# Layer 0 of a four-layer graph transformer: weight staging spread further, offset rows one product earlier, the experts' norm by chunks, and the experts' offsets in one fp16 product

## The chip, the cores and the metric

One core of one Trainium2 chip runs the whole program as one launch. The metric is the device time of that core in microseconds; lower is better. Times of the kernel are given as a median of runs, and one further execution was profiled.

## What is computed

Four layers run over x, 1250 rows (graph nodes) of 512 values, with 20000 edges. Each layer adds a graph part and an attention part to x, and then a mixture of experts. Only layer 0 is touched here:

```
xn = _layernorm(x, axis=-1)
x = x + _L0_gnn_ref(xn, edge_index, W, b) + _L0_mix_ref(xn[None], ...)[0]
x = x + _L0_ffn_ref(_layernorm(x, axis=-1)[None], ...)[0]

# _L0_mix_ref, for i in range(2):
    y = layernorm(x, ln1_g[i], ln1_b[i])
    ...                                   # attention with exponential features
    x = x + o @ Wo[i] + bo[i]
    y = layernorm(x, ln2_g[i], ln2_b[i])
    h = gelu(y @ W1[i] + b1[i])           # 512 -> 2048
    x = x + h @ W2[i] + b2[i]             # 2048 -> 512

# _L0_ffn_ref, 8 experts of 512 -> 128 -> 512, top 2, and one shared expert 512 -> 512 -> 512
scores = softmax(xf @ gate_w.T)
combine = top 2 of scores, normalised     # (tokens, 8)
eo = relu(xf @ w1 + b1) @ w2 + b2
y = einsum('te,teh->th', combine, eo)     # holds combine @ b2, the experts' offsets
shared = relu(xf @ sw1 + sb1) @ sw2 + sb2
```

## The kernel before

The 1250 rows lie as T = 10 tiles of 125 rows, and the tiles form three chunks, of 4, 4 and 2 tiles (CH). Each engine has its own program, written out by hand in the order in which it runs; semaphores connect them. A product in fp32 precision is made of three fp16 products, high x high, high x low and low x high (PARTS), so each operand is split into a high and a low fp16 half. `gemm_N` gives rows (12 matmuls of 512 columns for each tile, 120 in all, line L498), `gemm_T` gives columns (144 matmuls of 500 or 250 columns, line L480). TensorE (PE) writes into rings of three PSUM banks: the ring "act" is emptied by ScalarE (ACT), the ring "dve" by VectorE (DVE).

**Weights.** A weight matrix of 512x512 is a unit. SyncE (SP) loads it in four quarters into one of two `raw` slots, and GpSimd (POOL) splits each quarter (scale L2655, cast L2657, subtract L2659) into one of two unit slots. Unit u may be split when unit u-2 has been used. In layer 0: unit 4 is Wo of the first depth, 5 to 12 are its W1 and W2 in four pairs (b = 0 to 3), 16 is Wo of the second depth, 17 to 24 its W1 and W2; 25 to 28 are the experts' first and second matrices, four experts in a unit, 29 and 30 the shared expert's; 31 and on belong to layer 1.

**Staging.** The 50 expert units of layers 1 to 3 are split in the same way, ahead of time, and written back to memory: after unit u POOL splits SPLIT_AFTER[u] such units into four staging buffers in AT, and SP stores them. Since POOL works in program order, whatever is staged after unit u comes before the split of unit u+1. When the last is stored, SP brings the graph's adjacency back into AT (`adj_back`, 3.1 MB), which the gather of layer 1 reads; its loads stand in SP's queue ahead of the next unit's loads.

```
SPLIT_AFTER = {4: 9, 5: 9, 16: 9, 17: 9}
SPLIT_AFTER.update({u: 1 for u in [6, 7, 8, 9, 10, 11] + [18, 19, 20, 21, 22, 23, 24, 25]})
```

**End of each depth.** `add_to(M, "m_ffn", ...)` on DVE adds each bank of a gemm_N to the running stream M (L1850). In the last of the four (b = 3) it also adds the offset row b2 (L1853), in the second depth it adds M to X (L2140), and it takes the statistics of the row norm (L1793); after the last tile of a chunk DVE aggregates, ACT takes the root (L1395), DVE gives the scales. In the first depth (`beside_tiles`) PE transposes the first chunk ahead of tile 8 of the last product. Ahead of the experts it does not: `transposes_T` (L430) stands after the whole product, and on ACT `ln_root(Y)` norms all three chunks (L1426) before `evac_direct` empties the first bank (L1351). ACT copies the high halves (`hi_D`), DVE makes the low halves (`lo_D`, L1837).

**Experts.** PE multiplies three banks of unit 25, then the gate logits, then the rest. DVE turns the logits into `comb` in some 25 small steps (`gates`). PE transposes `comb` (10 transposes), and ten fp32 matmuls, combT (8 rows) times the offset rows E0, give the experts' offsets (L885), each emptied by DVE (`add_to(X, "read_dve")`, L1850). Then follows gemm_N with unit 26, whose banks come from the same ring of three.

Of the kernel before, what the change touches and what calls it, by code (L numbers as in the profile page):

```python
# [13 lines left out]
N = 1250  # L14
# [66 lines left out]
SEL = 9  # L81
MAX16 = 2048
# [5 lines left out]
def build(nc, x_in, src_in, dst_in, units_in, moe_in, be1_in, cols_in, rows_in, eb_in, gb2_in, proj_in, out):  # L88
    ctx = ExitStack()
    with ctx:  # L90
# [119 lines left out]
        combT = K[0:NE, N:2 * N]  # L210
# [173 lines left out]
        def _(pe):  # L384
# [49 lines left out]
            def normed_columns(c):  # L434
# [3 lines left out]
                for k in range(KC):  # L438
# [4 lines left out]
                    ins.then_inc(sem("filled_act"), 1)  # L443

# [248 lines left out]
            for dep in range(2):  # L693
# [107 lines left out]
                for b in range(4):  # L801
# [11 lines left out]
                    if b == 3:  # L813
                        uses_row()
# [3 lines left out]
                    else:  # L818
                        gemm_N("Q", lambda k, g: w[:, g, k, :], "m_ffn", by_chunk=True, between=beside_tiles if b == 3 and dep == 0 else None)
# [50 lines left out]
            def expert_biases(row):  # L870
# [3 lines left out]
                for t0, nt in CH:  # L874
                    pe.wait_ge(*left("act"))
                    o = bank("act", "combT")
                    for j in range(nt):
                        ins = pe.transpose(o[0:8, j * R:(j + 1) * R], comb3[:, t0 + j, :], ident[0:R, 0:R])
# [197 lines left out]
            transposes_T(lambda t, a, b: nat(Y, t, a, b), "normed", "lo_D")  # L1076
# [239 lines left out]
        def _(act):  # L1316
# [315 lines left out]
            def combT_evac():  # L1632
                for t0, nt in CH:
                    evac("act", "combT", combT[:, t0 * R:(t0 + nt) * R], nt * R, p=8)


            ln_root(Y)
            evac_direct("YT")
# [116 lines left out]
        def _(dve):  # L1755
# [268 lines left out]
            for dep in range(2):  # L2024
# [103 lines left out]
                for b in range(4):  # L2128
# [6 lines left out]
                    def stream_done(t):  # L2135

                        if dep == 0:
                            stream_rows(t)
                        else:
                            tt(nat(X, t), nat(X, t), nat(M, t), ALU.add).then_inc(sem("dve_step"), s.one("dve_step"))  # L2140
                            dve.wait_ge(*s.latest())
                            ln_scales(X, t)
                    add_to(M, "m_ffn", f"b2{dep}" if b == 3 else None, after=stream_done if b == 3 else None)
# [171 lines left out]
            def gates(probs, pair_softmax, gbias=False):  # L2315
# [45 lines left out]
                else:  # L2361
# [5 lines left out]
                    step(tt(comb3, w1, bc(mr), ALU.mult), "comb")  # L2367
                    step(ts(combs[0:R, :], comb[0:R, :], WS, None, ALU.mult))

# [8 lines left out]
            low_direct("YT")  # L2378
# [3 lines left out]
            row_free("E0")  # L2382
# [589 lines left out]
```

## Time and profile before

| | us |
|---|---|
| median of 3 runs | 3175.11 (3169.66 to 3175.34) |
| the profiled execution, its own time | 3171.26 |
| its span, first to last instruction | 3169.5 |
| TensorE busy | 2704.7 (85%) |
| VectorE busy | 1708.1 (54%) |
| GpSimd busy | 1193.4 (38%) |
| ScalarE busy | 1125.9 (36%) |
| mean granted TensorE clock | 0.921 of full speed |

The span is what the trace covers; 1.8 us of the execution's time lie around it. Busy shares are means over the whole span: an engine with 38% can still be the one that is waited for in one stage.

### The profile page before, as it was taken

The numbers are of one execution on the slowest core, as the hardware profiler recorded it, in microseconds if no ns is written. First come the engines' busy times: TensorE is split into PE (matmuls) and PEld (weight loads), VectorE is DVE, ScalarE is ACT, GpSimd is POOL, SyncE is SP. The second block draws the span as 40 slices with busy tenths as digits, with TensorE's granted clock in tenths as the row PEclk, the third lists the DMA queues.
The fourth block names the chain that finished last, engine by engine and source line by source line (L and its number), as shares of the span: only waits on it lengthen the run. The fifth ranks groups of instructions, "written<-read, shape, count | busy, mean of one in ns | idle before, by whom it ended". The sixth has DMA issues, their size and how long they took to land. (4 is left out here: it accounts for less than half of the span.)

```text
span 3169.5 us, 46348 instructions
## 1 busy us (share of the span) xinstructions
PE 2704.7 (85%) x17011; PEld 1760.6 (56%) x17011; DVE 1708.1 (54%) x3454; ACT 1125.9 (36%) x2510; POOL 1193.4 (38%) x1445
## 2 busy tenths in 40 slices
PE   8999899799889889899986956999599958589784
PEld 4655668456558646455544635777355645355453
DVE  8875878434678833655527253222435466541543
ACT  3254466233447522313214323444332235320132
POOL 2031677885377788623212212111003226300042
PEclk9999899999999999989997977999799979798887
DMA  2011445442154444411100007999601059600198
GB/s 63 1 51 37 126 144 160 139 130 80 47 153 147 153 134 131 136 33 34 37 11 27 31 15 286 416 417 414 200 4 38 21 210 322 211 14 0 33 365 271
DMA packets 163941, 415.35 MB, mean 131 GB/s; under 512 B 23931, under 2 KB 75675, under 8 KB 140236
## 3 DMA queue, kind: packets, MB, share of 16 engines
q1 hardware_dynamic: 149213, 362.10, 33.6%
q0 software_dynamic: 12960, 42.48, 3.5%
q10 hardware_dynamic: 1555, 7.95, 1.0%
q8 instruction: 132, 2.16, 0.3%
q14 instruction: 81, 0.66, 0.1%
HBM read 325.37 MB, written 87.09 MB: 130 GB/s over the span
## 5 line engine op out<-in xcount | busy, mean ns | idle before, releaser
L2655 POOL TENSOR_SCALAR raw<-raw 128x512 f32<-128x512 f32 x380 | 271.6, 715 | 1085.8 <-PE ps L480 434.7
L498 PE MATMUL ps<-units,ARENA 128*125 128x512 f16 x2880 | 643.9, 385 | 35.0 <-POOL units L2659 25.6
L480 PE MATMUL ps<-ARENA,units 128*128 128x500 f16 (+1 forms) x2952 | 537.5, 344 | 19.6 <-ACT tmp L1415 9.4
L498 PEld LDWEIGHTS ps<-units,ARENA 128*125 128x125 f16 x2880 | 391.1, 138 | 274.6 <-POOL units L2659 26.1
L480 PEld LDWEIGHTS ps<-ARENA,units 128*128 128x128 f16 x2952 | 289.2, 98 | 265.6 <-issue 19.0
L1813 DVE TENSOR_TENSOR ARENA<-tmp,ARENA 128x500 f16<-128x500 f32 (+3 forms) x241 | 173.1, 723 | 360.8 <-ACT ARENA L1341 187.6
L2659 POOL TENSOR_TENSOR AT<-raw,AT 128x512 f16<-128x512 f32 x200 | 243.9, 1220 | 17.0
L1340 ACT ACTIVATE tmp<-ps,cols 128x500 f32<-128x500 f32 (+1 forms) x156 | 95.7, 613 | 395.1 <-PE ps L480 385.3
L2703 POOL DMA_INDIRECT ARENA<-rows_d,proj x81 | 80.0, 987 | 389.0 <-DVE ARENA L2200 363.0
L2659 POOL TENSOR_TENSOR units<-raw,units 128x512 f16<-128x512 f32 x180 | 217.6, 1209 | 15.3
L2708 POOL DMA_INDIRECT picks_d<-ARENA,proj x81 | 82.1, 1014 | 345.1 <-DVE ARENA L2240 344.5
L973 PE MATMUL ps<-ARENA 128*128 128x128 f16 x3240 | 191.7, 220 | 0.1
L973 PEld LDWEIGHTS ps<-ARENA 128*128 128x128 f16 x3240 | 187.4, 98 | 1.5 <-DVE ARENA L2231 0.6
L988 PE MATMUL ps<-ARENA 128*128 128x512 f16 x810 | 184.2, 380 | 0.0
L1850 DVE SCALAR_TENSOR_TENSOR ARENA<-ps,ARENA 125x512 f32<-125x512 f32 x100 | 68.7, 687 | 153.6 <-PE ps L498 153.4
L430 PE MATMUL ps<-ident,ARENA 125*128 125x125 f32 x280 | 53.1, 352 | 111.8 <-DVE ARENA L1837 33.5
L1594 ACT ACTIVATE tmp<-ps,proj 128x128 f32<-128x128 f32 x270 | 102.6, 380 | 102.8 <-PE ps L973 72.7
L2657 POOL CAST AT<-raw 128x512 f16<-128x512 f32 x200 | 132.9, 664 | 12.8
L613 PE MATMUL ps<-ARENA 125*125 125x500 f16 (+1 forms) x588 | 118.6, 353 | 10.9 <-DVE ARENA L1915 9.9
L988 PEld LDWEIGHTS ps<-ARENA 128*128 128x128 f16 x810 | 74.8, 98 | 95.1 <-issue 12.2
L2240 DVE TENSOR_SCALAR ARENA<-ps,proj 128x512 f32<-128x512 f32 x81 | 60.7, 750 | 121.0 <-PE ps L988 76.9
L655 PE MATMUL ps<-proj,ARENA 128*125 128x256 f16 x640 | 106.0, 296 | 22.3 <-ACT AT L1526 11.4
(445 smaller groups left out, 4578.2 us busy)
## 6 DMA issues: line engine op xcount, KB each, us to landing
ARENA<-split_d SPq DMA_DIRECT2D x135, 1024.0 KB, 11.6
raw<-in_moe SPq DMA_DIRECT2D x200, 256.0 KB, 3.0
split_d<-AT SPq DMA_DIRECT2D x200, 256.0 KB, 2.5
raw<-in_units SPq DMA_DIRECT2D x180, 256.0 KB, 2.5
ARENA<-split_d SPq DMA_DIRECT2D x27, 1280.0 KB, 8.9
rows_d<-ARENA SPq DMA_DIRECT2D x6, 896.0 KB
ARENA<-picks_d SPq DMA_DIRECT2D x6, 896.0 KB
ARENA<-picks_d ACTq DMA_DIRECT2D x6, 896.0 KB
```

The source lines that it names most:

```text
L480: ins = pe.matmul(o[:, 0:nt * R], wt, mv_, start=(i == 0), stop=(i == len(steps) - 1))
L498: ins = pe.matmul(o[0:R, :], th(srcT, h, k, t, 1), w(k, g), start=(i == 0), stop=(i == len(steps) - 1))
L613: ins = pe.matmul(psA[b][0:R, 0:a1 - a0], ohd[j][:, 0:R], ohs[j][:, a0:a1], start=False, stop=False)
L655: ins = pe.matmul(o[0:R, h2 * NBF:(h2 + 1) * NBF], stack(2 * hp + h2, t, 1), features(dep, part), start=(part == 0), stop=(part == 1))
L973: ins = pe.matmul(o[:, oc * B:(oc + 1) * B], w1[:, gw, kk, oc * 128:(oc + 1) * 128], tile_T[g % 2][:, h, kk, :], start=(i == 0), stop=(i = ...
L988: ins = pe.matmul(o[:, :], tile_H[(g - 1) % 2][:, h, b * KC + kk, :], w2[:, gw, kk, :], start=False, stop=(b == halves - 1 and i == len(st ...
L1340: act.activation(tmp[:, i % STAGES, 0:width], o[:, 0:width], func, bias=bias, scale=scale)
L1594: act.activation(tmp[:, i % STAGES, oc * B:(oc + 1) * B], o[:, oc * B:(oc + 1) * B], func, bias=bias, scale=WS)
L1813: tt(lo, tmp[:, staged[0] % STAGES, 0:width], hi, ALU.subtract).then_inc(sem("lo_T"), s.one("lo_T"))
L2655: pool.tensor_scalar(r, r, WEIGHT_SCALE, 1.0, ALU.mult, ALU.mult).then_inc(sem("pool_step"), 1)
L2657: pool.tensor_copy(hi, r).then_inc(sem("pool_step"), 1)
L2659: pool.tensor_tensor(lo, r, hi, ALU.subtract).then_inc(sem(name), 1)
```

## The change

It has five parts, all in layer 0.

1. SPLIT_AFTER: 8 instead of 9 units are staged after units 4, 5, 16 and 17, and one each after units 26 to 29, which had none. The last staged unit is now behind unit 29 instead of 25, so the reload of the adjacency moves there too.
2. The offset row b2 of each depth is added beside the third W2 product (b = 2) instead of the fourth. In the second depth M goes into X there as well, and the fourth product is added straight to X.
3. The experts' norm goes by chunks: PE transposes chunk 0 ahead of tile 8 of the last product (`beside_direct`), ACT and DVE norm and empty chunk by chunk.
4. The experts' offsets: `comb` is laid out as 72 columns of parts (rounded at 0, rest at 32, rounded again at 64), the offset rows as 72 fp16 rows, so that one fp16 matmul takes the place of each fp32 one. DVE builds the offset rows (`offsets_in_parts`) ahead of `gates`, and the parts of `comb` inside it.
5. Row E0's slot is free after `offsets_in_parts` instead of after the addition.

```diff
-SPLIT_AFTER = {4: 9, 5: 9, 16: 9, 17: 9}
-SPLIT_AFTER.update({u: 1 for u in [6, 7, 8, 9, 10, 11] + [18, 19, 20, 21, 22, 23, 24, 25]})
+SPLIT_AFTER = {4: 8, 5: 8, 16: 8, 17: 8}
+SPLIT_AFTER.update({u: 1 for u in [6, 7, 8, 9, 10, 11] + [18, 19, 20, 21, 22, 23, 24, 25, 26, 27, 28, 29]})
...
-        combT = K[0:NE, N:2 * N]
+        combT = K[0:PART_ROWS, N:N + N // 2].bitcast(F16)
+        offset16 = K[0:PART_ROWS, 2 * N:2 * N + D // 2].bitcast(F16)
...
+            def direct_columns(c):
+
+                t0, nt = CH[c]
+                pe.wait_ge(sem("normed"), s.more("normed", nt))
+                for k in range(KC):
+                    pe.wait_ge(*left("act"))
+                    o = bank("act", "lo_D")
+                    for j in range(nt):
+                        ins = pe.transpose(o[:, j * R:(j + 1) * R], nat(Y, t0 + j, k * 128, (k + 1) * 128), ident[0:R, 0:R])
+                    ins.then_inc(sem("filled_act"), 1)
+
+            def beside_direct(t):
+
+                if t == 8:
+                    direct_columns(0)
...
-                    if b == 3:
+                    if b == 2:
                         uses_row()
...
-                pe.wait_ge(sem(f"row_loaded{ROWS.index(row) % ROW_SLOTS}"), 16 * (ROWS.index(row) // ROW_SLOTS + 1))
                 for t in range(T):
                     pe.wait_ge(*left("dve"))
                     o = bank("dve", "read_dve")
-                    pe.matmul(o[0:R, :], combT[:, t * R:(t + 1) * R], row_slots[0:8, ROWS.index(row) % ROW_SLOTS, :], start=True, stop=True).then_inc(sem("filled_dve"), 1)
+                    pe.matmul(o[0:R, :], combT[:, t * R:(t + 1) * R], offset16[:, :], start=True, stop=True).then_inc(sem("filled_dve"), 1)
...
-            transposes_T(lambda t, a, b: nat(Y, t, a, b), "normed", "lo_D")
+            direct_columns(1)
+            direct_columns(2)
             experts(2, 4, biases="E0", gate=0)
...
-            ln_root(Y)
-            evac_direct("YT")
+            norm_rows(0, X)
+            for c in range(2):
+                evac_direct("YT", groups=(4 * c, 4 * c + 3))
+                norm_rows(c + 1, X)
+                evac_direct("YT", groups=(4 * c + 3, 4 * c + 4))
+            evac_direct("YT", groups=(8, 12))
...
+                    def x_rows(t):
+
+                        ln_scales(X, t)
+                        if t in (7, 9):
+                            low_direct("YT", groups=(4 * (t - 7) // 2, 4 * (t - 7) // 2 + 4))
+
+                    if b == 2:
+                        add_to(M, "m_ffn", after=offset_rows)
+                        row_free(f"b2{dep}")
+                    elif b == 3:
+                        add_to(X if dep == 1 else M, "m_ffn", after=x_rows if dep == 1 else stream_rows)
+                    else:
+                        add_to(M, "m_ffn")
```

DVE, last W2 product of the second depth, its last tile and what follows, before the change (each row is one instruction, output<-inputs, and the size of the output):

```order
L1850 SCALAR_TENSOR_TENSOR ARENA<-ps,ARENA 125x512
L1853 TENSOR_TENSOR ARENA<-ARENA,row_slots 125x512
L2140 TENSOR_TENSOR X<-X,ARENA 125x512
L1793 BN_STATS stats<-X 125x6
L1799 BN_AGGR mv<-stats 125x2 x2
L1804 RECIPROCAL rstd<-std 125x2
L1806 SCALAR_TENSOR_TENSOR mv<-mv,rstd 125x2
L2146 MEMSET comb 125x10 x8
L1837 TENSOR_TENSOR ARENA<-ps,ARENA 128x500 x8
L1837 TENSOR_TENSOR ARENA<-ps,ARENA 128x250 x4
```

After the change, from the low halves of chunk 0 (L1861, four of them) over the last two tiles to the end:

```order
L1861 TENSOR_TENSOR ARENA<-ps,ARENA 128x500 x4
L1874 SCALAR_TENSOR_TENSOR X<-ps,X 125x512
L1817 BN_STATS stats<-X 125x6
L1874 SCALAR_TENSOR_TENSOR X<-ps,X 125x512
L1817 BN_STATS stats<-X 125x6
L1823 BN_AGGR mv<-stats 125x2 x2
L1828 RECIPROCAL rstd<-std 125x2
L1830 SCALAR_TENSOR_TENSOR mv<-mv,rstd 125x2
L1861 TENSOR_TENSOR ARENA<-ps,ARENA 128x500 x4
L2183 MEMSET comb 125x10 x8
L1861 TENSOR_TENSOR ARENA<-ps,ARENA 128x250 x4
```

A tile's four instructions have become two, and the low halves of chunks 0 and 1 stand ahead of tile 8 and right behind tile 9 instead of all at the end.

PE, from the last W2 product to the experts' first product, before:

```order
L498 MATMUL ps<-units,ARENA 125x512 x120
L430 MATMUL ps<-ident,ARENA 128x125 x40
L480 MATMUL ps<-ARENA,units 128x500 x36
L827 MATMUL ps<-gates,ARENA 125x16
```

and after:

```order
L518 MATMUL ps<-units,ARENA 125x512 x96
L457 MATMUL ps<-ident,ARENA 128x125 x16
L518 MATMUL ps<-units,ARENA 125x512 x24
L457 MATMUL ps<-ident,ARENA 128x125 x24
L500 MATMUL ps<-ARENA,units 128x500 x36
```

Sixteen of the forty transposes have moved ahead of the product's last two tiles.

SP, the end of the staging, after the change (raw<-in_units are loads of a unit's quarters, raw<-in_moe loads of staged quarters, split_d<-AT their stores, AT<-adj_d the reload):

```order
L2898 DMA raw<-in_units 128x512 x3
L2927 DMA raw<-in_moe 128x512 x2
L2853 DMA split_d<-AT 256x1x512
L2927 DMA raw<-in_moe 128x512
L2853 DMA split_d<-AT 256x1x512
L2927 DMA raw<-in_moe 128x512
L2853 DMA split_d<-AT 256x1x512 x2
L2939 DMA AT<-adj_d 112x6250
L2940 DMA AT<-adj_d 112x80
L2898 DMA raw<-in_units 128x512 x4
```

The same sequence stood behind unit 25 and ahead of unit 26 before; it now stands behind unit 29 and ahead of unit 30, the second matrix of the shared expert.

## Rows read from the trace of the kernel before

**Rows 1.** The page, part 2: granted TensorE clock in 40 slices.

```profile
PEclk9999899999999999989997977999799979798887
```

**Rows 2.** Waits of PE: line, releaser, total us, times, longest.

```profile
PE ps L498 <- POOL units L2659: 25.6, 2, 13.1
```

**Rows 3.** Timeline of PE, two depths: start, us, instructions [idle before, releaser].

```profile
605.04 28.88 PE L498 MATMUL ps<-units,ARENA 128*125 128x512 f16 x120 [12.49 <-POOL units L2659]
...
1137.27 29.00 PE L498 MATMUL ps<-units,ARENA 128*125 128x512 f16 x120 [13.09 <-POOL units L2659]
...
1191.49 26.06 PE L498 MATMUL ps<-units,ARENA 128*125 128x512 f16 x120
```

**Rows 4.** Windows: busy us of PE, PEld, DVE, ACT, POOL, clock, DMA, GB/s.

```profile
605.00:610.00 5.00, 4.96 (x12) 2.79 (x13) 0.00 (x0) 0.00 (x0) 4.19 (x6) 0.50 0.35 101
```

**Rows 5.** Timeline of POOL, first and last instruction of 36 staged quarters.

```profile
471.48 0.62 POOL L2655 TENSOR_SCALAR raw<-raw 128x512 f32<-128x512 f32 x1 [0.23 <-DMA raw<-in_moe]
...
591.44 1.20 POOL L2659 TENSOR_TENSOR AT<-raw,AT 128x512 f16<-128x512 f32 x1
```

**Rows 6.** Timeline of PE and DVE, end of the first depth.

```profile
800.87 6.92 PE L480 MATMUL ps<-ARENA,units 128*128 128x500 f16 x24 [3.89 <-ACT tmp L1415]
...
811.25 17.09 PE L480 MATMUL ps<-ARENA,units 128*128 128x500 f16 x96
...
791.64 1.62 DVE L1853 TENSOR_TENSOR ARENA<-ARENA,row_slots 125x512 f32<-125x512 f32 x1
...
794.62 1.58 DVE L1853 TENSOR_TENSOR ARENA<-ARENA,row_slots 125x512 f32<-125x512 f32 x1
```

**Rows 7.** Timeline of PE, from the last W2 product to the experts.

```profile
1322.17 1.45 PE L430 MATMUL ps<-ident,ARENA 125*128 125x125 f32 x12
1336.32 5.42 PE L430 MATMUL ps<-ident,ARENA 125*128 125x125 f32 x24 [12.70 <-DVE ARENA L1837]
...
1342.88 7.76 PE L480 MATMUL ps<-ARENA,units 128*128 128x500 f16 x36
```

**Rows 8.** DVE, L1850 from 1200 us, the others at the end: ns min/median/max.

```profile
L1850 DVE SCALAR_TENSOR_TENSOR ARENA<-ps,ARENA x28: 672/691/692, 1199.5 to 1329.7; 125x512 f32<-125x512 f32 x28
...
L1853 DVE TENSOR_TENSOR ARENA<-ARENA,row_slots x10: 691/906/1585, 1297.7 to 1330.4; 125x512 f32<-125x512 f32 x10
...
L2140 DVE TENSOR_TENSOR X<-X,ARENA x10: 691/980/1532, 1298.4 to 1331.1; 125x512 f32<-125x512 f32 x10
...
1299.52 0.69 DVE L1793 BATCH_NORM_STATS2 stats<-X 125x6 f32<-125x512 f32 x1
```

**Rows 9.** Timeline of ACT, norm of chunk 1 and the first banks emptied.

```profile
1327.01 2.93 ACT L1426 ACTIVATE ARENA<-X,mv,rstd 125x512 f32<-125x512 f32 x4 [0.44 <-DVE mv L1806]
...
1334.99 1.51 ACT L1351 ACTIVATE ARENA<-ps 128x500 f16<-128x500 f32 x3
```

**Rows 10.** Timeline of PE and DVE, the experts' offsets.

```profile
1379.88 15.29 PE L885 MATMUL ps<-row_slots,ARENA 8*125 8x512 f32 x20 [0.80 <-ACT ARENA L1322]
...
1381.90 0.69 DVE L1850 SCALAR_TENSOR_TENSOR X<-ps,X 125x512 f32<-125x512 f32 x1 [0.17 <-PE ps L885]
```

**Rows 11.** Timelines of SP, POOL and PE, staging, reload and the next unit.

```profile
1326.38 0.34 SPq L2883 DMA_DIRECT2D AT<-adj_d  x1
...
1310.98 0.62 POOL L2655 TENSOR_SCALAR raw<-raw 128x512 f32<-128x512 f32 x1
...
1322.66 1.16 POOL L2659 TENSOR_TENSOR AT<-raw,AT 128x512 f16<-128x512 f32 x1
...
1345.14 0.62 POOL L2655 TENSOR_SCALAR raw<-raw 128x512 f32<-128x512 f32 x1 [19.06 <-DMA raw<-in_units]
...
1354.38 1.15 POOL L2659 TENSOR_TENSOR units<-raw,units 128x512 f16<-128x512 f32 x1
...
1449.17 0.62 POOL L2655 TENSOR_SCALAR raw<-raw 128x512 f32<-128x512 f32 x1 [13.10 <-PE ps L480]
...
1501.63 26.06 PE L498 MATMUL ps<-units,ARENA 128*125 128x512 f16 x120
```

More of the change, by code:

```diff
@@ L818, in _ @@
                     else:
-                        gemm_N("Q", lambda k, g: w[:, g, k, :], "m_ffn", by_chunk=True, between=beside_tiles if b == 3 and dep == 0 else None)
+                        gemm_N("Q", lambda k, g: w[:, g, k, :], "m_ffn", by_chunk=True, between=beside_tiles if b == 3 and dep == 0 else beside_direct if b == 3 else None)
                     free(u, "dve")
@@ L2134, in _, with offset_rows @@
                         low_parts("Q", "hT")
[L2135 to L2139, printed above, removed]
[L2140 to L2143 removed]
+                    offset = row(f"b2{dep}") if b == 2 else None
+                    def offset_rows(t):
+                        tt(nat(M, t), nat(M, t), offset, ALU.add).then_inc(sem("dve_step"), s.one("dve_step"))
+                        if dep == 1:
+                            dve.wait_ge(*s.latest())
+                            tt(nat(X, t), nat(X, t), nat(M, t), ALU.add).then_inc(sem("dve_step"), s.one("dve_step"))
+                    def x_rows(t):
[9 more added lines that the diff above has]
+                        add_to(M, "m_ffn")
             for e in range(NE):
@@ L2366, in gates, with offsets_in_parts @@
                     step(tt(w1, w1, lg, ALU.mult))
-                    step(tt(comb3, w1, bc(mr), ALU.mult), "comb")
-                    step(ts(combs[0:R, :], comb[0:R, :], WS, None, ALU.mult))
+                    step(tt(comb3, w1, bc(mr), ALU.mult))
+                    step(dve.tensor_copy(comb16, comb3))
+                    for p in (0, 64):
+                        dve.tensor_copy(comb_parts[:, :, p:p + NE], comb16)
+                    step(tt(comb_parts[:, :, 32:32 + NE], comb3, comb16, ALU.subtract), "comb")
+                    step(ts(combs[0:R, :], comb[0:R, :], WS, None, ALU.mult))
+            def offsets_in_parts():
+                e = row("E0")
+                ins = dve.memset(offset16[:, :], 0.0)
+                ins.then_inc(sem("dve_step"), s.one("dve_step"))
+                dve.wait_ge(*s.latest())
+                for p in (0, 32):
+                    ins = dve.tensor_copy(offset16[p:p + NE, :], row_slots[p:p + NE, ROWS.index("E0") % ROW_SLOTS, :])
+                ins.then_inc(sem("dve_step"), s.one("dve_step"))
+                dve.wait_ge(*s.latest())
+                tt(offset16[64:64 + NE, :], e[0:NE, :], offset16[0:NE, :], ALU.subtract).then_inc(sem("dve_step"), s.one("dve_step"))
+                row_free("E0")
+                dve.memset(comb_parts[:, :, :], 0.0).then_inc(sem("dve_step"), s.one("dve_step"))
+                dve.wait_ge(*s.latest())
             def expert_sum(e):
@@ L2375, in expert_sum @@
                     stt(nat(X, t), o[0:R, :], combs[0:R, t * NE + e:t * NE + e + 1], nat(X, t), ALU.mult, ALU.add).then_inc(sem("read_dve"), s.one("read_dve"))
-            low_direct("YT")
+            low_direct("YT", groups=(8, 12))
+            offsets_in_parts()
             gates(True, False)
```

8 lines of the change are left out of this document (5 added, 3 removed).

## Prediction

> **What bounds the kernel now.** First the page: TensorE is busy 85% of the span, and its granted clock is at or near full in most slices [rows 1], so time is won where PE stands still, where its clock falls after that, or where it multiplies in fp32. Then the waits of PE: its rows product waits for POOL's split twice, 25.6 us in all [rows 2]. PE's timeline puts one wait into each depth, 12.49 and 13.09 us, ahead of the first W2 product (units 6 and 18), and that product then takes 28.88 and 29.00 us where an undisturbed one takes 26.06 [rows 3]; the window behind the wait shows why, a granted clock of 0.50, the lower of the two levels, for 5 us [rows 4]. Third, the end of the second depth: PE does three banks of transposes and stands still for 12.70 us, until the low halves of DVE come [rows 7]. Last, the ten fp32 products for the offsets take 15.29 us [rows 10]. The change touches each of these, so I sum it place by place. All the sums are made on the profiled execution.
>
> **Part 1, staging, the waits.** POOL's timeline shows 36 staged quarters from 471.48 to 592.64, 3.37 us each [rows 5], and unit 6 is split behind them. Two blocks of 9 units become two of 8, so eight quarters fewer stand ahead of unit 6: 8 x 3.37 = 27 us earlier, against a wait of 12.49. Unit 6 must also wait until unit 4 has been used, but POOL worked on staging until 592.64, so the slot was not what held it. The wait goes, with 14 us to spare, and with it the slow start of the product: 12.49 + (28.88 - 26.06) = 15.3. In the second depth likewise 13.09 + (29.00 - 26.06) = 16.0 [rows 3]. Next late would be unit 7: POOL now has it 14 us sooner than PE asks for it. Bounds: 25.6 if the clock falls anyway, 31.3 as taken.
>
> **Part 1, staging, what it costs later.** Four units are now staged beside the experts. A unit's split takes 10.4 us (1345.14 to 1355.53), a staged one 12.8 (1310.98 to 1323.82) [rows 11], together 23.2 against the 26.06 us of one product, so POOL keeps up for units 27 to 29. Unit 30 is another matter, since the reload is now ahead of its loads in SP's queue. Unit 29 is split from 1449.17, when unit 27 is free. Add 10.4 for it, 12.8 for the staged one, 2.6 until the reload starts (1323.82 to 1326.38 before), 18.8 from there to the first quarter of the next unit (to 1345.14, where POOL's row names the load as what it waited for) and 10.4 for its split: 1504.1. PE wants it at 1501.63 [rows 11]. So a new wait of 2.5 us. Bounds: 0, if the staged unit goes faster beside a quieter DVE, and 8, if it and the reload each take some 3 us more. What the reload covered before was PE's own standstill at 1323 to 1336 [rows 7]. The gather that reads the adjacency starts only after the 26 us of unit 30's product, so it isn't reached.
>
> The page "DMA: Bandwidth & Descriptors" of the Trainium skill, section "Bandwidth", gives 425 GB/s for a large load; an estimate from it is 3.1 MB in about 7.3 us instead of 18.8, so that unit 30 would be ready 9 us ahead of PE and the sum would be 2.5 us larger. The row of this trace is for the very same transfer, so I stay with it.
>
> **Part 2, the offset rows.** In the first depth each of the last two tiles loses an addition of 1.62 and 1.58 us on DVE; PE waits 3.89 us for what hangs on these tiles (statistics, root, norm, columns by ACT), and its next 24 matmuls take 6.92 us [rows 6] where 36 of the same form take 7.76 at full clock [rows 7], 5.2 for 24. The chain comes 3.2 to 3.7 us sooner, so the wait nearly goes, and some of the 1.7 us of slow clock, and some of the 17.09 us of the next 96. But behind it DVE and ACT make heads at their own pace, so not all of it stays. I take 4.5; bounds 3 and 6.5. The additions themselves now stand beside the third product, where in the first depth DVE has one more of 0.69 us for each tile. In the second depth it has two more: by the medians 0.69 + 0.91 + 0.98 + 0.09 between them = 2.67 us a tile [rows 8] against PE's 2.6. It ends some 2 us behind PE, and the first three blocks of the next product (7 us) need only free banks from ACT, which holds three results for DVE. So 0; the upper bound is in the rivals.
>
> **Parts 2 and 3, the end of the second depth.** A tile on DVE is now 0.69 + 0.69 = 1.4 us instead of some 3.3 [rows 8], PE gives one each 2.6 us, and the two short waits behind tiles 7 and 8 (1.7 us) go, while four banks of transposes (2.1) come in; the product still ends at about 1322.3. Going through it: tile 7 leaves PE two tiles and four banks earlier, at 1322.3 - 5.2 - 2.1 = 1315.0, and DVE has chunk 1's statistics 1.4 + 0.4 later, with the hand-over at 1317; ACT has then emptied three banks of chunk 0, takes the root and norms four rows in 2.93 [rows 9], to 1321.6, and empties the fourth by 1322.2. DVE makes that low half by 1322.9, then tiles 8 and 9 until 1325.6, the aggregate until 1326.0. ACT's root, DVE's scales and two rows of ACT (1.5) end at 1328.6. PE, which has transposed chunk 1 by 1324.6, then does chunk 2; with ACT emptying a bank in 0.5 to 0.6 [rows 9], the experts' first product starts at 1330.3 instead of 1342.88 [rows 7]. That is 12.6. PE still idles 4 us, so the product may start at the lower clock, which cost 1.7 on 24 matmuls in [rows 6, 7]: I take 1.3 off, so 11.3; bounds 8 and 12.6. The logits are asked for after three more banks (7.8 us), when all low halves are there; `offsets_in_parts`, 5 short DVE instructions of at most 0.7 each, fits ahead of that.
>
> **Part 4, the offsets.** The ten fp16 products cost 2 to 3 us on PE, but each bank must be emptied by DVE: 0.69, and 0.17 between where the bank was there first [rows 10]. The first matmul of unit 26 needs the bank of the eighth offset: 8 x 0.72 to 0.86 = 5.8 to 6.9 us, and 0.4 for the first. So it starts 6.2 to 7.3 after 1379.88 instead of 15.2 after it: 7.9 to 9.0, I take 8.4. Bound below: 5, if each hand-over costs 0.4 more. The extra steps in `gates` (four of 0.24 us) delay the low halves by about 1 us, while PE has banks to go on with: 0. The parts of comb are made while PE still has several blocks of unit 25 to multiply, so they aren't waited for.
>
> **The sum.** 15.3 + 16.0 + 4.5 + 11.3 + 8.4 - 2.5 = 53.0. From the profiled execution's 3171.26 that gives 3118.3. The median of the runs shown is 3.9 above that execution, which would be 3122.1. I say 3120.
>
> **Rivals.**
> - *VectorE becomes the bound in the third product.* The largest additions in [rows 8] are 1.59 and 1.53 us, beside a busy POOL; if each took that, a tile is 3.9 us, ten are 39, and the second depth loses about 12: sum 41, 3132. For it: POOL is busier there than at the end. Against it: the medians. The page "SBUF — State Buffer", section "Who interferes with whom", says that a `tensor_tensor` with both inputs in SBUF takes the port pair that GpSimd needs and that the loser blocks fully; by that rule the maxima would be the usual case. The spread of the rows, 0.69 to 1.59, agrees that it happens, and the median that it is not the usual case.
> - *The reload holds unit 30 longer*, by 8 to 15 us, since the transfer now shares the queue with stores that end later: 3126 to 3133.
> - *The norm's standstill stays*, because `low_direct` now stands ahead of tile 8 on DVE and waits for ACT: if that costs what the chunking gains, 4 of the 11.3 are left: 3127.
> - *Unit 6 is still late*: another thing than the 8 quarters holds it. Then each depth keeps up to its wait: 3136 to 3150. Against it: POOL shows no wait for PE there [rows 5].
> - *Slower than before.* Place: staging beside the experts. POOL has 26.06 - 10.4 = 15.7 us for a staged unit before PE waits; each us above that is paid four times, and the reload's wait comes on top. To lose the 55.5 us of gains, a staged unit must take (55.5 - 2.5)/4 + 15.7 = 29 us, 7.2 a quarter. The rows show 3.2 and 3.37.
> - *Nothing happens*: the gains only move PE's waits to a place further on, such as the next release by POOL. Against it: the 23.2 us of POOL's work in each 26.06.
>
> **How the numbers follow.** The forecast 0.62, VectorE the bound 0.09, the reload 0.10, the norm 0.09, unit 6 late 0.05, slower 0.02, nothing 0.02, an offset part below its bound 0.01. The sum of the lower bounds of the certain parts, 25.6 + 3 + 8 + 5 - 8 = 34, is 3137 to 3141; that of the upper, 31.3 + 6.5 + 12.6 + 9, is 59, 3112 to 3116, and a little clock may come on top. The range 3108 to 3138 takes both in and the first four rivals. About 0.2% (6 us) is what a measurement of this kernel can tell from no change. Faster by more 0.96, within it 0.02, slower 0.02.
>
> **What would show it.** PE's first W2 product of each depth has no wait for POOL and takes 26.1; if a wait stays, the count of quarters is not the cause. PE's last wait before the experts is 4 us, not 12.7, and the first product begins 12 us sooner after the last W2 product. The offsets span about 7 us, with DVE's instructions end to end. PE waits 2 to 3 us for POOL ahead of unit 30, and POOL for the load. DVE's additions beside the third product are 0.7 to 1.0. The prediction is wrong if PE waits for DVE there, or if the reload is slower beside the experts' work.

## The result and the profile after

| | us |
|---|---|
| the changed kernel, median of 4 runs | 3121.3 (3115.47 to 3129.92) |
| the kernel before, 4 runs, one of them new | 3172.39 (3166.62 to 3175.34) |
| ratio after to before, 95% interval | 0.9843 (0.9815 to 0.9872) |
| profiled execution, its own time | 3121.03 |
| its span | 3119.3 |

The kernel is 1.6% faster. The profiled execution stands 50.2 us below the one of before; 3120 was said, within 3108 to 3138, and the sum on the profiled execution was 3118.3.

The page of the changed kernel; the last row is the granted clock in 40 slices, beside [rows 1]:

```profile
span 3119.3 us, 46337 instructions
...
PE 2688.9 (86%) x17001; PEld 1753.1 (56%) x17001; DVE 1713.3 (55%) x3463; ACT 1122.7 (36%) x2510; POOL 1195.4 (38%) x1445
...
PEclk9999899999999999999989968999899989698797
```

PE's busy time fell by 15.8 us (2704.7 to 2688.9), which is slow clock behind the waits and the fp32 products of the offsets; the other 34 of the 50 us are standing still that went. I read the rest place by place, in the order of the program.

**Waits for POOL.** The wait group of PE that answers to [rows 2], and PE's timeline at the first W2 product of each depth and at unit 30, beside [rows 3]:

```profile
PE ps L518 <- POOL units L2715: 1.4, 1, 1.4
```

```profile
592.24 26.06 PE L518 MATMUL ps<-units,ARENA 128*125 128x512 f16 x120
...
1104.60 26.06 PE L518 MATMUL ps<-units,ARENA 128*125 128x512 f16 x120
...
1447.83 26.11 PE L518 MATMUL ps<-units,ARENA 128*125 128x512 f16 x120 [1.40 <-POOL units L2715]
```

Neither W2 product has an idle time in brackets any more, and both take 26.06 us. A window at the start of the first shows a granted clock of 1.00 (2.4 GHz), where [rows 4] had 0.50 (1.2 GHz) behind the wait:

```profile
592.00:597.00 5.00, 5.00 (x27) 3.24 (x26) 1.87 (x3) 0.83 (x2) 4.09 (x6) 1.00 0.48 155
```

From POOL's timeline, its last instruction on unit 6; PE asks for the unit 16.6 us after this one ends:

```profile
574.19 1.46 POOL L2715 TENSOR_TENSOR units<-raw,units 128x512 f16<-128x512 f32 x1
```

**End of the first depth**, PE, beside [rows 6]:

```profile
781.84 2.71 PE L500 MATMUL ps<-ARENA,units 128*128 128x500 f16 x12 [0.47 <-ACT tmp L1435]
...
792.22 16.33 PE L500 MATMUL ps<-ARENA,units 128*128 128x500 f16 x96
```

The wait of 3.89 us is now 0.47.

**End of the second depth**, PE from the last W2 product to the transposes of comb, beside [rows 7]. Bracketed times are waits; the two ahead of L457 are for low halves of DVE:

```profile
1258.46 20.88 PE L518 MATMUL ps<-units,ARENA 128*125 128x512 f16 x96
1279.18 1.45 PE L457 MATMUL ps<-ident,ARENA 125*128 125x125 f32 x12
1282.77 0.65 PE L457 MATMUL ps<-ident,ARENA 125*128 125x125 f32 x4 [2.14 <-DVE ARENA L1861]
1283.25 5.34 PE L518 MATMUL ps<-units,ARENA 128*125 128x512 f16 x24
1288.43 1.45 PE L457 MATMUL ps<-ident,ARENA 125*128 125x125 f32 x12
1291.88 0.65 PE L457 MATMUL ps<-ident,ARENA 125*128 125x125 f32 x4 [2.00 <-DVE ARENA L1861]
...
1295.08 9.85 PE L500 MATMUL ps<-ARENA,units 128*128 128x500 f16 x36
...
1332.11 1.49 PE L898 MATMUL ps<-ident,ARENA 125*72 125x125 f32 x10
```

One wait of 12.70 us has become two of 2 us. The same 36 matmuls take 9.85 us where they took 7.76 (mean granted clock 0.79 over 1295 to 1305 us), so some slow clock has come along.

**The offsets**, PE and DVE, beside [rows 10]:

```profile
1334.40 0.86 PE L904 MATMUL ps<-ARENA 72*125 72x512 f16 x3 [0.80 <-ACT ARENA L1342]
...
1336.81 3.08 PE L904 MATMUL ps<-ARENA 72*125 72x512 f16 x5 [0.17 <-DVE X L1874]
...
1339.89 28.47 PE L518 MATMUL ps<-units,ARENA 128*125 128x512 f16 x120
```

```profile
1334.87 6.07 DVE L1874 SCALAR_TENSOR_TENSOR X<-ps,X 125x512 f32<-125x512 f32 x10 [0.94 <-PE ps L904]
```

Unit 26's product follows 5.5 us after the first offset's matmul, not 15.2. DVE is the pace: PE's matmuls wait for it, and it makes ten additions end to end in 6.07 us.

**The reload**, SP and POOL around unit 30, beside [rows 11]; the first and third row of POOL are the first quarters of units 29 and 30. Then windows over the reload (the last two columns are the DMA share and GB/s):

```profile
1418.53 0.34 SPq L2939 DMA_DIRECT2D AT<-adj_d  x1
...
1393.83 0.62 POOL L2711 TENSOR_SCALAR raw<-raw 128x512 f32<-128x512 f32 x1 [1.78 <-PE ps L500]
...
1404.42 0.62 POOL L2711 TENSOR_SCALAR raw<-raw 128x512 f32<-128x512 f32 x1 [0.32 <-DMA raw<-in_moe]
...
1436.46 0.62 POOL L2711 TENSOR_SCALAR raw<-raw 128x512 f32<-128x512 f32 x1 [20.48 <-DMA raw<-in_units]
```

```profile
1418.00:1425.00 7.00, 7.00 (x34) 3.36 (x33) 4.14 (x8) 1.24 (x2) 0.00 (x0) 1.00 0.84 225
1425.00:1437.00 12.00, 12.00 (x59) 5.50 (x57) 3.37 (x5) 5.69 (x10) 0.54 (x1) 1.00 0.83 179
```

**Where the gain arises.** Starts of the same PE instruction, before minus after, add up from left to right: 15.62 us behind unit 6, 19.8 at the end of the first depth (step 4.2), 35.6 behind unit 18 (15.8), 35.6 still at the last W2 product, 45.5 at the transposes of comb (9.9), 55.2 at unit 26 (9.7), 53.8 at unit 30 (-1.4). The end of the span is only 50.2 earlier, although layers 1 to 3 are the same code; more on that below.

These sums compare one execution with one. The same program was profiled once more (e10), and there PE is at unit 30 only 47.6 us earlier (1501.63 - 1454.01):

```profile
595.37 26.06 PE L518 MATMUL ps<-units,ARENA 128*125 128x512 f16 x120
...
1454.01 26.11 PE L518 MATMUL ps<-units,ARENA 128*125 128x512 f16 x120 [1.79 <-POOL units L2715]
```

Of the 6.2 us between the two, 3.1 lie already ahead of unit 6 (595.37 for 592.24) and 2.7 between the end of the first depth and unit 18; from there to unit 30 the two agree within 0.4. It is scatter, since the program is the same.

### The profile page after: what moved, and what is told of

It is laid out like the page before. It is cut to its first block and busy times, and to the rows that moved or that the text cites. A ratio compares the mean times of both kernels' runs of the same rounds, so it can differ in the third digit from the quotient of the medians.

```text
span 3119.3 us, 46337 instructions
## 1 busy us (share of the span) xinstructions
PE 2688.9 (86%) x17001; PEld 1753.1 (56%) x17001; DVE 1713.3 (55%) x3463; ACT 1122.7 (36%) x2510; POOL 1195.4 (38%) x1445
## 5 line engine op out<-in xcount | busy, mean ns | idle before, releaser
L518 PE MATMUL ps<-units,ARENA 128*125 128x512 f16 x2880 | 636.0, 382 | 9.1 <-DVE ARENA L1861 5.3
L2715 POOL TENSOR_TENSOR units<-raw,units 128x512 f16<-128x512 f32 x180 | 221.3, 1229 | 15.3
L2713 POOL CAST AT<-raw 128x512 f16<-128x512 f32 x200 | 134.5, 672 | 12.8
L434 PE MATMUL ps<-ident,ARENA 125*128 125x125 f32 x240 | 46.1, 355 | 98.0 <-ACT ARENA L1446 27.4
L2713 POOL CAST units<-raw 128x512 f16<-128x512 f32 x180 | 123.6, 687 | 11.5
```

Source lines behind the costliest of these rows:

```text
L518: ins = pe.matmul(o[0:R, :], th(srcT, h, k, t, 1), w(k, g), start=(i == 0), stop=(i == len(steps) - 1))
L2713: pool.tensor_copy(hi, r).then_inc(sem("pool_step"), 1)
L2715: pool.tensor_tensor(lo, r, hi, ALU.subtract).then_inc(sem(name), 1)
```

## Experiments

Four stretches of PE's timeline tell the parts apart. S1: from the last W2 product of the first depth to the 96 matmuls that follow its norm. S2: from the last W2 product of the second depth to the transposes of comb. S3: from there to unit 26's product. S4: from the long group in unit 28's product to unit 30's product. Then the waits for POOL ahead of units 6, 18 and 30, and the ratio of the runs to those of the kernel before on the same chip (intervals about 0.0025 to either side). In e4's trace the group at which S4 begins is not separate.

| kernel | S1 | S2 | S3 | S4 | POOL waits | ratio |
|---|---|---|---|---|---|---|
| before | 49.5 | 83.6 | 17.5 | 50.2 | 12.5, 13.1, 0 | 1 |
| changed | 46.1 | 73.7 | 7.8 | 51.7 | 0, 0, 1.4 | 0.9843 |
| e1 staging only | 49.6 | 84.6 | 17.0 | 54.1 | 0, 0, 3.8 | 0.9934 |
| e2 staging back | 46.1 | 76.9 | 7.8 | 50.2 | 12.9, 9.8, 0 | 0.995 |
| e3 columns behind | 46.1 | 73.9 | 7.8 | 52.1 | 0, 0, 1.8 | 0.9853 |
| e4 offsets fp32 | 46.1 | 74.6 | 17.6 | - | 0, 0, 3.4 | 0.9878 |
| e5 row in fourth | 50.3 | 87.8 | 7.8 | 52.1 | 0, 0, 1.8 | 0.9898 |
| e6 two units moved | 46.1 | 75.9 | 7.8 | 50.2 | 0, 0.7, 0 | 0.9868 |
| e7 bank later | 46.1 | 73.6 | 7.8 | 52.7 | 0, 0, 2.4 | 0.986 |
| e8 both | 46.1 | 73.5 | 7.8 | 50.2 | 1.1, 0.7, 0 | 0.9842 |
| e9 staged behind 12 to 15 | 49.0 | 73.9 | 7.8 | 50.2 | 0, 0, 0 | 0.9861 |
| e10 changed again | 46.1 | 73.6 | 7.8 | 52.1 | 0, 0, 1.8 | 0.9859 |
| e11 as e9, bank later | 49.0 | 73.1 | 7.8 | 50.2 | 0, 0, 0 | 0.9864 |
| e12 staged behind 12, 13 | 46.2 | 74.0 | 7.8 | 50.2 | 0, 0, 0 | 0.9852 |

How far a stretch scatters is seen where the code is the same: S2 was 73.6 to 76.9 in seven kernels (changed, e2, e4, e6, e9, e10, e12). S1 agrees within 0.1 among the kernels with the change's code there, but for e9 and e11 (below), and S3 too; the old code of S3 took 17.5 in one execution and 17.0 in another (e1). Part 5 was undone only together with part 4 (e4).

### Each part undone or alone

e1 takes only the two SPLIT_AFTER lines of the diff, e2 takes only these back. e3 (lines cut):

```diff
-                        gemm_N("Q", lambda k, g: w[:, g, k, :], "m_ffn", by_chunk=True, between=beside_tiles if b == 3 and dep == 0 else beside_direct if b == 3 else None)
+                        gemm_N("Q", lambda k, g: w[:, g, k, :], "m_ffn", by_chunk=True, between=beside_tiles if b == 3 and dep == 0 else None)
...
-            direct_columns(1)
-            direct_columns(2)
+            for c in range(3):
+                direct_columns(c)
...
-            norm_rows(0, X)
-            for c in range(2):
-                evac_direct("YT", groups=(4 * c, 4 * c + 3))
-                norm_rows(c + 1, X)
-                evac_direct("YT", groups=(4 * c + 3, 4 * c + 4))
-            evac_direct("YT", groups=(8, 12))
+            for c in range(3):
+                norm_rows(c, X)
+            evac_direct("YT")
...
-                        if t in (7, 9):
-                            low_direct("YT", groups=(4 * (t - 7) // 2, 4 * (t - 7) // 2 + 4))
...
-            low_direct("YT", groups=(8, 12))
+            low_direct("YT")
```

e4 (lines cut; `gates`, the transposes of comb and their copies go back to eight columns likewise, and the row's slot is freed behind the addition again):

```diff
-        combT = K[0:PART_ROWS, N:N + N // 2].bitcast(F16)
+        combT = K[0:NE, N:2 * N]
...
-                    pe.matmul(o[0:R, :], combT[:, t * R:(t + 1) * R], offset16[:, :], start=True, stop=True).then_inc(sem("filled_dve"), 1)
+                    pe.matmul(o[0:R, :], combT[:, t * R:(t + 1) * R], row_slots[0:8, ROWS.index(row) % ROW_SLOTS, :], start=True, stop=True).then_inc(sem("filled_dve"), 1)
...
-            offsets_in_parts()
```

> The kernel before with part 1 of the change alone (SPLIT_AFTER). Theory (separate places that add up): both waits for POOL ahead of the W2 products go, with the slow clock behind them, 15.6 + 15.7 us as the trace of after has it, and PE waits some 1.5 us for POOL ahead of unit 30: about 30 us less than before, ratio 0.9906 (0.989 to 0.992). The norm's standstill of 12.7 us and the 15.3 us of offsets stay. Rival (reload): before, the reload of the adjacency was covered by PE's standstill at the norm, which is still there, so if the place behind unit 29 is what costs, the wait ahead of unit 30 is 1.4 us here too, and not larger. Rival (the gains only move PE's waits on): under 20 us less.

> The changed kernel with the old SPLIT_AFTER. Theory: the two waits for POOL come back at 12.5 and 13.1 us, each with a product of some 29 us behind it, and the wait ahead of unit 30 goes: about 30 us more than the changed kernel, so ratio to before 0.994 (0.992 to 0.995). Rival (parts interact): since the offset row and the norm no longer hold PE in the last products, PE asks POOL earlier for unit 16 and 18 and the waits grow by what parts 2 and 3 gave: then depth 1's wait is 13.1 + 4.2 = 17.3 us, and the first depth's gain of 4.2 us is lost again.

> The changed kernel with part 3 undone: PE transposes all three chunks behind the last product, ACT norms all of them before it empties the first bank, DVE makes the low halves at the end. The offset row stays in the third product. Theory (part 2 carries most of the gain at the end of the second depth, since DVE was behind by its three additions a tile): the standstill of PE ahead of the experts is about 6.4 us, not 12.7, and the experts' first product starts 2.5 us later than in the changed kernel (1.2 to 4.5). Total 2.5 us more. Rival (the norm by chunks carries it): it starts 8 to 10 us later and the standstill is 10 to 12 us.

> The changed kernel with part 4 undone: the experts' offsets as ten fp32 products of 8 rows. Theory: from the first of the ten to unit 26's product 15.2 us instead of 5.5, so about 9.7 us more than the changed kernel, and unit 30 is asked for that much later, so PE's wait of 1.4 us ahead of unit 30 stays as it is, because unit 29's split starts when unit 27 is free and moves along. Rival (DVE's preparation of the parts was itself in the way): the logits' path gets shorter by up to 1 us and the difference is 8.7 us or less.

e1, PE; the standstill at the norm and unit 30:

```profile
1308.75 5.67 PE L430 MATMUL ps<-ident,ARENA 125*128 125x125 f32 x24 [14.22 <-DVE ARENA L1837]
...
1478.27 27.77 PE L498 MATMUL ps<-units,ARENA 128*125 128x512 f16 x120 [3.77 <-POOL units L2659]
```

Staging alone takes both waits away, but pays 3.8 us and a slower product (27.77 for 26.06) at unit 30, more than the 1.4 expected. Its profiled span is 17.1 us below that of before, its ratio 0.9934 (0.9908 to 0.9961) is 21 us (12 to 29), where 30 was expected. The ratio expected was 0.9906 (0.989 to 0.992), so this expectation was missed. In the profiled execution the missing 13 are found: 3.0 up to the last W2 product, of which 2.5 lie ahead of unit 6 in code that is not touched; 1.1 more in S2, 0.5 less in S3; 2.9 more than expected up to the start of unit 30's product (3.8 us of wait among it); and 6.3 from there to the end, of which 1.7 are that product's slow clock and the rest lies in code that is untouched. How the untouched parts stood in its other runs stays open. The ratios of e1 and e2 put the staging and the rest at 21 and 16 us, 37 together for 50; their intervals (12 to 29, 8 to 23) just allow it, so the parts are told apart by the stretches and not by the totals.

e2, PE, the two waits that come back:

```profile
604.32 28.73 PE L518 MATMUL ps<-units,ARENA 128*125 128x512 f16 x120 [12.85 <-POOL units L2715]
...
1130.94 28.25 PE L518 MATMUL ps<-units,ARENA 128*125 128x512 f16 x120 [9.75 <-POOL units L2715]
```

They do not grow by what parts 2 and 3 give, and S1 keeps its gain: that rival falls. POOL's own work is tied to PE's releases of units and moves with them: behind the first depth its next two splits wait for PE in both kernels and start at 824.17 and 853.77 us here, 828.44 and 858.04 before. The second wait is even 3.3 us shorter. So these waits carry some 3 us of scatter in a single execution. The ratio, 0.995 for 0.994, is as expected.

e3, PE behind the last W2 product:

```profile
1286.82 1.45 PE L457 MATMUL ps<-ident,ARENA 125*128 125x125 f32 x12
1292.23 3.97 PE L457 MATMUL ps<-ident,ARENA 125*128 125x125 f32 x20 [3.97 <-DVE ARENA L1858]
...
1298.46 7.76 PE L500 MATMUL ps<-ARENA,units 128*128 128x500 f16 x36
...
1334.80 1.49 PE L898 MATMUL ps<-ident,ARENA 125*72 125x125 f32 x10
```

With the norm whole again the standstill is 3.97 us and not 12.70, less than the 6.4 expected; the experts' product starts 0.9 us later than in the changed kernel (2.5 expected, 1.2 to 4.5), but its 36 matmuls have the full clock, and at comb 0.2 us are left. Beside e10, whose 36 matmuls had the full clock too, it starts 0.3 us later. The norm by chunks is worth nothing measurable. The standstill was DVE's: with two additions a tile less, it is done in time either way. Which of the two (the offset row, M to X) weighs how much was not tried.

e4, PE:

```profile
1335.16 15.41 PE L905 MATMUL ps<-row_slots,ARENA 8*125 8x512 f32 x20 [0.80 <-ACT ARENA L1343]
...
1350.50 28.49 PE L518 MATMUL ps<-units,ARENA 128*125 128x512 f16 x120
```

S3 is 17.6, 9.8 us more, which is what undoing part 4 (with part 5) gives back; the preparation of the parts costs nothing that PE sees (S2 is 74.6, within its scatter). PE's wait ahead of unit 30 was 3.4 us, not the 1.4 expected.

### The offset row back in the fourth product

```diff
-                    if b == 2:
+                    if b == 3:
                         uses_row()
...
+                    def offset_and_rows(t):
+
+                        offset_rows(t)
+                        dve.wait_ge(*s.latest())
+                        (x_rows if dep == 1 else stream_rows)(t)
```

> The changed kernel with the offset rows (and in the second depth M to X) back in the fourth W2 product; the norm by chunks stays. The run with part 3 undone gave up only 0.2 us, from 73.65 us between the last W2 product and the comb transposes to 73.88, against 83.56 before. Theory now (DVE's three additions a tile made the standstill, not the order of the norm): here those 73.65 us go back to 83.6 or more, up to 90, since the low halves of chunks 0 and 1 (8 x 0.69 us) now stand on a DVE that is already behind PE by 0.7 us a tile; and the first depth loses its 4.2 us again. Total 14 to 20 us more than the changed kernel. Rival (the norm by chunks is worth as much by itself, either part will do): those 73.65 us grow by no more than 3 us, total under 8 us more.

PE, around tiles 8 and 9 of the last W2 product:

```profile
1298.99 1.10 PE L457 MATMUL ps<-ident,ARENA 125*128 125x125 f32 x4 [10.10 <-DVE ARENA L1861]
...
1314.10 2.07 PE L457 MATMUL ps<-ident,ARENA 125*128 125x125 f32 x8 [5.25 <-DVE ARENA L1861]
```

The norm by chunks without part 2 makes S2 87.8 us, 3 to 4 more than without either (84.6 in e1, 83.6 before): PE now waits for DVE's low halves in the middle of a product, and the 24 matmuls behind that wait take 7.68 us where they take 5.34 in the changed kernel. Three us are also what S2 scatters by, so the loss is seen in one execution and not proven; that the chunks alone gain nothing is plain. S1 is back at 50.3. Its ratio, 0.9898, is 17 us more than the changed kernel's, 12 more than e10's; 14 to 20 were expected. The gain of both ends belongs to the moved additions.

### Where to stage

e6 and e8 use `{4: 9, 5: 8, 16: 9, 17: 8}` with one unit each behind 26 and 27; e9 and e11 use 8 each, with one behind 12 to 15; e12 8 each, with one behind 12, 13, 26 and 27. e7, e8 and e11 also move the fourth bank of chunk 0 (lines cut; `direct_columns` takes the banks as an argument):

```diff
                 if t == 8:
-                    direct_columns(0)
+                    direct_columns(0, range(0, 3))
+                if t == 9:
+                    direct_columns(0, range(3, 4))
```

> The changed kernel with SPLIT_AFTER 9, 8, 9, 8 for units 4, 5, 16, 17 and one each behind 26 and 27 only: four quarters fewer ahead of unit 6 and of unit 18 instead of eight, and the reload behind unit 27. Theory (only the count of quarters ahead of the W2 unit governs its wait): 4 x 3.37 = 13.5 us sooner against waits of 12.49 and 13.09, so both are gone or under 1 us (up to 2.5 in one execution, since POOL's staging ran up to 3 us faster or slower between executions); the wait of 1.4 us ahead of unit 30 goes, since comb and the offsets give POOL 8 us of slack ahead of unit 28. Total 1.5 us less than the changed kernel (3 less to 1 more). Rival (the reload holds the unit behind it wherever it is placed): PE waits 1.4 to 4 us ahead of unit 28 instead.

> The changed kernel with the fourth bank of chunk 0's transposes moved from ahead of tile 8 to ahead of tile 9. The changed kernel's PE waits there 2.14 us for DVE's low half, which alone frees a bank. Theory: that wait goes and nothing else moves, since DVE's low halves of chunk 0 are made from the same banks in the same place: 36.62 us from the last W2 product to the experts' first become 34.5 to 35.5, and 1 to 2 us less in all, inside what the runs' spread can tell but plain in the trace. Rival (the end is set by DVE and ACT behind tile 9, as the run without part 3 suggests, where PE stood still elsewhere and lost only 0.2 us): the wait behind chunk 1 grows by what is won here, 0 us.

> The two edits of the runs with two units moved and with the fourth bank later, together. If they add up as each theory has it, 2.5 to 3.5 us less than the changed kernel: about 3118 where that is 3121. If both rivals hold, no change.

e6, PE:

```profile
1106.08 26.11 PE L518 MATMUL ps<-units,ARENA 128*125 128x512 f16 x120 [0.74 <-POOL units L2715]
...
1449.32 26.06 PE L518 MATMUL ps<-units,ARENA 128*125 128x512 f16 x120
```

Half the quarters moved takes 13.5 us from waits of 12.5 and 13.1 and leaves 0 to 1.1 us (e6, e8), as counted. PE no longer waits ahead of unit 30, nor ahead of unit 28, though the reload now stands ahead of that: comb and the offsets give POOL the time there.

e7, PE:

```profile
1292.32 0.65 PE L458 MATMUL ps<-ident,ARENA 125*128 125x125 f32 x4 [0.38 <-DVE ARENA L1864]
...
1300.12 0.65 PE L458 MATMUL ps<-ident,ARENA 125*128 125x125 f32 x4 [3.29 <-DVE ARENA L1864]
```

The wait of 2.14 falls to 0.38, the next grows from 2.00 to 3.29, and S2 stays: the rival was right, the end is set behind tile 9. e8, both edits together, is no faster either (0.9842).

> The changed kernel with the four single staged units behind units 12 to 15 (where POOL of the kernel before stood idle for 16 to 27 us ahead of each) instead of 26 to 29, so the reload of the adjacency stands behind unit 25 again. Theory (the reload holds up the unit behind it by some 55 us of POOL and DMA work against two products, unless PE has a pause there; comb and the offsets are that pause): no wait ahead of unit 30, where the runs so far had 1.4, 1.8, 3.8 and 2.4 us and up to 1.7 us of slow clock; from unit 28's product to unit 30's 50.2 us instead of 51.7 to 54.1; none ahead of units 6, 18 and 27; total 1.5 to 4 us less than the changed kernel. Rival (POOL's slack in the attention part is needed: unit 16 and the eight units staged behind it come 12.8 us later): then PE waits again ahead of unit 18, up to 13 us, and it is slower than the changed kernel.

> The changed kernel once more, unaltered, to stand beside the others on the same chip. Theory: the same stretches as in its first trace wherever PE waits for on-chip work (offsets 7.8 us, first depth's end 46.1 us), and a ratio of 0.984 to 0.987 to before. From the last W2 product to the comb transposes the four kernels with the same code there showed 73.65 to 76.9 us, and from there to unit 30 the wait was 1.4 to 3.4: so 73.5 to 77 and 1.4 to 3.8 us here.

> The staging of the run before this one (behind units 12 to 15) and the fourth bank of chunk 0 ahead of tile 9. The bank alone gave 0 in the trace (73.64 and 73.52 us to the comb transposes against 73.65), so by that the time is that of the earlier staging alone; 1 us less if the slow stretches of 74.6 to 76.9 us in three of the runs come from the wait that this edit takes away.

e9, PE; S4 is 50.2 as expected, but S1 is 2.9 us longer:

```profile
800.67 18.20 PE L500 MATMUL ps<-ARENA,units 128*128 128x500 f16 x96 [1.97 <-ACT tmp L1435]
```

Groups of DVE in that place (us in all, mean ns of one), first e9, then e10:

```profile
L2029 DVE TENSOR_TENSOR ARENA<-tmp,ARENA 64x500 f16<-64x500 f32 x4 | 5.0, 1262 | 0.1
L2028 DVE TENSOR_TENSOR ARENA<-tmp,ARENA 64x500 f16<-64x500 f32 x4 | 4.4, 1108 | 0.1
```

```profile
L2029 DVE TENSOR_TENSOR ARENA<-tmp,ARENA 64x500 f16<-64x500 f32 x4 | 2.7, 676 | 0.1
L2028 DVE TENSOR_TENSOR ARENA<-tmp,ARENA 64x500 f16<-64x500 f32 x4 | 2.7, 673 | 0.1
```

The same instructions take 1.1 to 1.3 us on average instead of 0.67 while POOL splits the unit staged behind 14. PE never waits for POOL there; its 1.97 us are for ACT, and ACT waits for DVE, which is slow beside POOL:

```profile
799.97 0.56 ACT L1435 ACTIVATE tmp<-ps,cols 128x250 f32<-128x250 f32 x1 [2.00 <-DVE ARENA L2029]
```

e11 repeats it (49.0). In e10 S2 (73.6), the wait (1.8) and the ratio (0.9859) came out as expected.

> The changed kernel with the four single staged units behind 12, 13, 26 and 27. In the run with 12 to 15 the unit staged behind 14 ran on POOL beside the eight head instructions of VectorE at the end of the first depth, which took 0.96 to 1.54 us each instead of 0.67, and the first depth's end took 49.0 us instead of 46.1. Those behind 12 and 13 stood beside the fourth W2 product, which was none the slower. Theory (a staged unit costs what it takes from VectorE where PE waits for VectorE, and the reload costs only where PE has no pause for it): the first depth's end is 46.1 us again, no wait ahead of unit 28 or 30, and 50.2 us from unit 28's product to unit 30's instead of 51.7 to 54.1. Total 1.5 to 4 us less than the changed kernel. Rival (any staged unit in that stretch costs): the first depth's end stays at 48 to 49 us and the total is that of the changed kernel.

e12, PE:

```profile
794.07 17.91 PE L500 MATMUL ps<-ARENA,units 128*128 128x500 f16 x96
```

S1 is 46.2, S4 50.2, and POOL is not waited for in layer 0's products at all: the mechanism holds. In the total, 1.5 us and some slow clock are too little: 3123.93 us and 0.9852 (0.9824 to 0.9879), beside 0.9843 and 0.9859 of the changed kernel. None of e6 to e12 is measurably faster than the change: the 1 to 4 us expected of some of them are less than these intervals can tell (0.0025 is 8 us), and no ratio shows them.

**Where the totals scatter.** From the start of unit 30's product to the end of the span it is 1671.5 us in the changed kernel, 1667.8 in e10, which is the same program, 1660.7 in e6 and 1676.4 in e12; before it was 1667.9. The code is the same in all. These 16 us are more than the differences between e3 and e6 to e12, and 3.6 of them are why the span gained 50.2 and not 53.8.

## Why the prediction was right, and where its sizes were off

- **Waits ahead of units 6 and 18: right.** 15.3 and 16.0 said, 15.6 and 15.8 measured, the clock with them. That they fit so closely is in part luck: e10, the same program, shows 12.5 at the first place, since PE came there 3 us later. Unit 6 was ready 29.3 us sooner (575.65 for 605.0), said 27. e1 and e2 show that it is SPLIT_AFTER alone, e6 and e8 that it goes by the count of quarters.
- **Unit 30: right in kind, 1.4 us for 2.5.** From unit 29's first quarter: split 10.6, staged unit 11.6 (12.8 said), 2.5 to the reload, 17.9 (18.8 said) to the first quarter, 11.4 (10.4 said): 54.0 against the 52.6 after which PE asks. (The staged unit ends with SP's last store, issued at 1416.0.) The wait was 1.4 to 3.8 us in seven kernels with this placement, around what was said; from the reload's start to the next unit's first quarter they took 17.7 to 19.0.
- **The page "DMA: Bandwidth & Descriptors", section "Bandwidth", of the Trainium skill** states its 425 GB/s for a transfer of 16 MB; by the prediction's estimate from it (7.3 us) there would have been no wait. The trace disagrees for this transfer of 3.1 MB: 17.9 us, at 225 and 179 GB/s in the two windows, though the page of the profile shows other slices at 412 to 416.
- **End of the first depth: right.** 4.5 said, 4.2 measured, of it 3.4 in S1 and the rest clock; e5 gives S1 back.
- **Third product, second depth: right in cost, wrong in duration.** 0 said and measured, but from a tile of 2.67 us on DVE that came from medians of another place. It is 1.20 + 1.06 + 0.68 = 2.94 us without the gaps, against PE's 2.6. The groups of DVE there, in the changed kernel, and its read of the last tile's bank:

```profile
L2163 DVE TENSOR_TENSOR ARENA<-ARENA,row_slots 125x512 f32<-125x512 f32 x10 | 12.0, 1200 | 0.3
L2166 DVE TENSOR_TENSOR X<-X,ARENA 125x512 f32<-125x512 f32 x10 | 10.6, 1061 | 0.3
L1874 DVE SCALAR_TENSOR_TENSOR ARENA<-ps,ARENA 125x512 f32<-125x512 f32 x10 | 6.8, 682 | 1.0 <-PE ps L518 1.0
...
1236.87 0.68 DVE L1874 SCALAR_TENSOR_TENSOR ARENA<-ps,ARENA 125x512 f32<-125x512 f32 x1
```

PE had finished that product at 1233.23 (1207.17 + 26.06), so DVE was 3.6 us behind, less than the two tiles (5.2 us) that the ring's other banks give it, and PE never stood still. The rival "VectorE becomes the bound" was closer than its 9 in 100. The page "SBUF — State Buffer" of the Trainium skill, section "Who interferes with whom", says that a VectorE instruction with two inputs in SBUF contends with a GpSimd instruction that reads SBUF, and one with at most one such input, outside its two-port modes, does not. These rows and those of e9 agree, and the addition from PSUM (L1874) keeps its 0.68. The prediction has it that the loser blocks fully; the page calls the contention an exclusive lock and says so in these words only of the two-port modes. In this product no addition took more than 1.62 us, against 0.69 alone.

- **End of the second depth: 11.3 said, 9.9 measured, and put down to the wrong part.** The experts' product starts 12.2 us sooner (12.6 said), though not by the steps that I walked through: a bank of the ring is free only when DVE has taken its low half, so PE stands for 2.14 us ahead of tile 8 and 2.00 behind the product. The slow clock took 2.1 us of the first 36 matmuls, 1.3 said (none in e10). The failed step is the attribution: I went through it as the merit of both parts, and e3 shows 0.2 us for the chunks, e5 that alone they gain nothing and may cost 3 to 4. The additions that moved are the whole term. The prediction's rival that the norm's standstill stays, if `low_direct` costs what the chunks gain, had 4 of the 11.3 left; the chunks' gain did come to nothing, but the additions alone carried 9.7.
- **The offsets: 8.4 said, 9.7 measured.** Direction and pace-setter (DVE) right; a bank costs 0.61 us, not 0.72 to 0.86, since each addition that follows another without a wait starts before that one's recorded end (ten in 6.07 us, though one alone shows 0.68).
- **The sum:** 53.0 said, 53.8 at unit 30. Errors of +1.3 (offsets), +1.1 (unit 30) and -1.4 (norm) nearly cancel, and e10 has 47.6 where this execution has 53.8: that the sum was met within 1 us is luck; by e10 it would have been missed by 5. What the total then showed, 50.2, also holds 3.6 us of scatter in unchanged code.

## What to carry to other kernels

When PE stands still at a norm, first add up what the adding engine does per tile against PE's time per tile. Moving the additions to a product behind which nothing waits for them was worth about 10 us at one norm and 4 at the other, the rearranged norm nothing, and where the additions stayed it gained nothing either. Background work on an idle engine is placed by what it takes from others: behind unit 14 it cost 2.9 us, through VectorE, without any wait for POOL. And attribute with a kernel that lacks one part, reading the stretch in the trace: totals scattered by more than most of the parts were worth.

## What was not expected of the hardware

- VectorE's additions and subtractions with both inputs in SBUF took 1.06 to 1.26 us beside a busy GpSimd, on the average and not only at the worst, and 0.67 to 0.69 alone.
- A wait of PE for another engine came back in the clock only in part of the cases: the same 36 matmuls took 7.76 us in e3 (behind 3.97 us of waiting at once) and in e10 (behind 2.83 and 2.00), 9.85 in the changed kernel (behind 2.14 and 2.00) and 8.5 in e7. What decides it these runs don't show.
